# Cross-attention and routed feed-forward on one core: another order of the first transfers, all first norms on VectorE, and a query stack with its group axis first

## What is computed

```python
x = x + cross_attention(layernorm(x), ctx, ctx, mask)     # 16 heads of 8, scores clipped to +-50, no maximum taken
x = x + moe(layernorm(x))                                 # 8 experts, the best 2 of each token, 128 -> 512 -> 128, gelu

q = layernorm(x) @ W_q.T;  k = ctx @ W_k.T;  v = ctx @ W_v.T
p = exp(clip(q k / sqrt(8)));  attention = (p v / sum(p)) @ W_o.T
```

## Time and profile before

| | |
|---|---|
| median of 3 runs | 1106.81 us (1106.25 to 1107.64) |
| the profiled execution | 1106.66 us, its span 1104.9 us |
| mean granted clock of TensorE | 0.969 of full speed |
| PE busy | 1033.4 us, 94% of the span |
| ACT, DVE, POOL busy | 769.6, 761.0, 240.0 us |
| chain that ended last, PE's share | 90% |

### The profile page before, as it was taken

The page is one execution under the profiler, slowest core; times in us unless marked ns, Lnnn a source line. Parts: engine busy times, 40 slices in busy tenths (PEclk is TensorE's granted clock), DMA queues, the critical chain, the costliest instruction groups (busy, mean ns, idle before and its releaser), DMA issues.

```text
span 1104.9 us, 32396 instructions
## 1 busy us (share of the span) xinstructions
PE 1033.4 (94%) x10544; PEld 759.8 (69%) x10545; DVE 761.0 (69%) x2088; ACT 769.6 (70%) x1088; POOL 240.0 (22%) x320
## 2 busy tenths in 40 slices
PE   5789999999999999999999999999999999399990
PEld 3567677777777677777677777777767776299990
DVE  4567777777777777777777777777777777444433
ACT  2567877777777877777877777877778777144430
POOL 3331111111111111111111111111111111245554
PEclk8899999999999999999999999999999999699995
DMA  7645555455555554555455555555555544022216
GB/s 217 186 154 166 173 170 170 165 166 167 168 171 170 172 171 164 173 167 170 167 171 173 173 173 173 174 174 174 174 174 174 174 157 142 23 68 63 65 49 178
DMA packets 144319, 172.71 MB, mean 156 GB/s; under 512 B 32235, under 2 KB 88559, under 8 KB 144287
## 3 DMA queue, kind: packets, MB, share of 16 engines
q1 hardware_dynamic: 138622, 165.26, 45.4%
q0 software_dynamic: 4896, 6.63, 2.2%
q10 hardware_dynamic: 768, 0.41, 0.2%
HBM read 36.83 MB, written 22.08 MB: 53 GB/s over the span
## 4 chain that ended last, share of the span: by engine, by line
PE 90%; DMA 3%; POOL 2%; SPq 2%; DVE 1%; issue 1%; ACT 1%; ACTq 0%; POOLq 0%; DVEq 0%
PE scores L753 31%; PE o_sum L765 26%; PE scratch L687 7%; PE scratch L676 7%; PE scores L873 5%; PE scores L884 5%; PE scratch L671 4%; PE scratch L726 1%; SPq L535 1%; POOL w_sb L597 1%; PE scratch L681 1%; PE scratch L731 1%; DMA x_all<-in_x_dram 1%; DMA q_stack<-q_rep 1%; PE scratch L747 1%
## 5 line engine op out<-in xcount | busy, mean ns | idle before, releaser
L990 ACT ACTIVATE probs<-scores 128x800 f32<-128x800 f32 (+1 forms) x640 | 615.2, 975 | 160.7 <-PE scores L753 158.6
L753 PE MATMUL scores<-q_stack,k_stack 128*128 128x400 f32 x1536 | 415.2, 380 | 10.5 <-DMA q_stack<-q_rep 8.1
L1136 DVE TENSOR_SCALAR probs<-probs 128x800 f32<-128x800 f32 (+1 forms) x640 | 396.2, 654 | 25.2 <-ACT probs L990 25.0
L753 PEld LDWEIGHTS scores<-q_stack,k_stack 128*128 128x128 f32 x1536 | 249.2, 190 | 110.5 <-issue 100.9
L765 PE MATMUL o_sum<-probs,v_both 128*17 128x200 f32 x6144 | 316.3, 335 | 0.1
L765 PEld LDWEIGHTS o_sum<-probs,v_both 128*17 128x17 f32 x6144 | 151.1, 97 | 132.4 <-issue 71.9
L630 POOL DMA_INDIRECT expert_rows<-rows,row_atu x64 | 75.6, 1181 | 408.8 <-DVE row_atu L1233 361.4
L687 PE MATMUL scratch<-w_turned,ctxT 128*128 128x128 f32 x768 | 102.5, 277 | 0.0
L687 PEld LDWEIGHTS scratch<-w_turned,ctxT 128*128 128x128 f32 x768 | 101.2, 194 | 0.0
L1073 DVE COPY v_both<-scratch 128x512 f32<-128x512 f32 x93 | 64.4, 692 | 42.4 <-PE scratch L687 42.4
L1048 DVE CAST k_hi<-k_full 128x512 fp32r<-128x512 f32 (+1 forms) x93 | 38.4, 412 | 79.5 <-ACT k_full L932 79.4
(11 more groups left out here) (145 smaller groups left out, 771.1 us busy)
## 6 DMA issues: line engine op xcount, KB each, us to landing
k_stack<-k_hi SPq DMA_DIRECT2D x192, 256.0 KB, 2.5
k_stack<-k_lo SPq DMA_DIRECT2D x192, 256.0 KB, 2.6
expert_rows<-fill SPq DMA_DIRECT2D x32, 406.2 KB
xT_and_ctx<-in_ctx_dram SPq DMA_DIRECT2D x16, 704.0 KB
ctx_nat<-in_ctx_dram SPq DMA_DIRECT2D x16, 704.0 KB
q_rep<-q_parts SPq DMA_DIRECT2D x124, 50.0 KB, 1.9
q_stack<-q_rep SPq DMA_DIRECT2D x124, 50.0 KB, 1.9
v_both<-expert_rows SPq DMA_DIRECT2D x57, 65.0 KB, 1.8
```

Source lines behind the costliest of these rows:

```text
L753: last = nc.tensor.matmul(score_banks(c)[:, m, :], k_stack[p][:, g, t * P:(t + 1) * P], q_stack[p][:, :, g, :], start=True, stop=True)
L990: nc.scalar.activation(probs_of(c), score_banks(c), ACT.Exp, scale=SCALE).then_inc(exp_ready, 1)
L1136: nc.vector.tensor_scalar(chunk, chunk, LOW, HIGH, ALU.max, ALU.min).then_inc(probs_ready, 1)
```

## The change

Four things change. `x` comes in parts of 1, 3 and 4 groups in place of 2, 2 and 4. The transfers of the last third of the first keys and of the last part of `x` are issued behind the spreading of the second query, which waits for the first query's stacking. The norms of groups 4, 5 and 7 move from POOL to DVE, and the chunks in which DVE takes the late moments and norms are other ones. And `q_stack` has its axes as (group, head, query) where it had (head, group, query), so that the 400 columns of one group lie side by side for each matmul and each partition's part of a stacking transfer lies in four places.

```diff
-    DVE_NORMS = [0, 1, 2, 3, 6]
-    POOL_NORMS = [4, 5, 7]
...
-    X_PARTS = [(0, 2), (2, 4), (4, QSTEPS)]
-    LATE_MOMENTS = {3: 4, 4: 5, 5: 6, 7: 7}
-    LATE_NORMS = {10: 6}
+    X_PARTS = [(0, 1), (1, 4), (4, QSTEPS)]
+    LATE_MOMENTS = {4: 4, 6: 5, 8: 6, 11: 7}
+    LATE_NORMS = {7: 4, 9: 5, 11: 6, 14: 7}
...
-        q_stack = [sb(f"q_stack{p}", [P, HG, GROUPS, SQ], F32R) for p in range(2)]
+        q_stack = [sb(f"q_stack{p}", [P, GROUPS, HG, SQ], F32R) for p in range(2)]
...
-            def stack_keys(p, b):
+            def stack_keys(p, b, thirds=range(KSTEPS)):
 
-                for k in range(KSTEPS):
+                for k in thirds:
...
-                    sp.dma_start(q_stack[p][h * R:(h + 1) * R, h, :, :].bitcast(F32),
+                    sp.dma_start(q_stack[p][h * R:(h + 1) * R, :, h, :].bitcast(F32),
                                  q_rep[h * R:(h + 1) * R, :, :].bitcast(F32)).then_inc(q_stacked, 16)
...
             sp.wait_ge(cleared, 3)
-            stack_keys(0, 0)
+            stack_keys(0, 0, (0, 1))
+            spread_queries(1)
+            stack_keys(0, 0, (2,))
             load_x(2)
-            spread_queries(1)
...
-            for r in range(2, 4):
+            for r in range(2, QSTEPS):
                 invert_deviations(r)
-
-            def late_norm(r):
...
-                if r in DVE_NORMS:
-                    pe.wait_ge(normed_ready, QB * (DVE_NORMS.index(r) + 1))
-                else:
-                    pe.wait_ge(normed_ready_pool, QB * (POOL_NORMS.index(r) + 1))
+                pe.wait_ge(normed_ready, QB * (r + 1))
...
-                                            q_stack[p][:, :, g, :],
+                                            q_stack[p][:, g, :, :],
```

More of the change, by code:

```diff
@@ L306, in xattn_moe @@
         normed_ready = sem("normed_ready")
-        normed_ready_pool = sem("normed_ready_pool")
         w_in_psum = sem("w_in_psum")
@@ L966, in stack_first @@
                 for h in range(HG):
-                    act.dma_start(q_stack[0][h * R:(h + 1) * R, h, :, :].bitcast(F32),
+                    act.dma_start(q_stack[0][h * R:(h + 1) * R, :, h, :].bitcast(F32),
                                   q_rep[h * R:(h + 1) * R, :, :].bitcast(F32)).then_inc(q_stacked, 16)
```

## The result

The changed kernel took 1098.68 us in the median of 4 runs (1096.85 to 1099.86) against 1106.53 us of the kernel before beside it; the ratio is 0.9926 with an interval of 0.9909 to 0.9943. It is faster by 7.9 us, where 22.6 were forecast. The profiled execution took 1099.86 us, within 0.4 us of the first rival's 1100.2.

A forecast was written before the change was run, and what follows sets the result against it. PE was taken to bound the kernel, 90% of the span by the chain. From 1106.66 us, 6.5 us at the start and 16.1 us in the score matmuls came off, giving 1084.1 us; the forecast's own range was 1077 to 1095.

The forecast's parts named there:

- the first rival: Score matmuls stay at 0.185 us because the excess belongs to operand type or weights; layout idle; 1100.2 us, chance 0.36.
- the term of 16.1 us: Steady part: 1488 score matmuls each 0.012 us shorter through the new layout, 17.9 us, less a tenth.
- The query stack: Prediction's section on `q_stack`'s new axes: stacking transfers cost nothing more, score matmuls gain 16.1 us.
- the three jumps: Score matmuls read 400 columns in four pieces; without the jumps between them the distance falls 0.014 us, to 0.171 us.
- The start: Up to the second sequence: first scores at 26.9 us instead of 33.80, second sequence at 62.9 instead of 69.38.
- The term of 6.5 us: Gain at the second sequence's start from the earlier first scores; bounds 1.0 to 8.8 us.
- The first part of `x`: Halving `x` part 0 lands it sooner, so the first query follows 1.2 us earlier; bounds 0 and 2.
- Each us of landing behind 38.9 us is one us of time: First sequence: later landing of `x` part 2 costs time one for one, as DVE's 16.9 us follow whole.
- those 16.9 us: DVE's work from `x` part 2's landing at 38.9 us to the clipping of chunk 11, at 55.8 us.
- The second rival: First sequence: late `x` part 2 makes DVE wait longer than the start won; landing at 50 us gives 1111 us; chance 0.05.

The follow-up runs named there:

- the early `x` part: Changed kernel with `x` part 2 issued once the first query is stacked, ahead of second query's spreading and last third of keys: 1094.39 us.
- The bf16 kernel: Changed kernel with all score matmuls on two fixed bf16 tiles of zeros, 400 columns: 1049.33 us.
- the one with zeros in `F32R`: Changed kernel with all score matmuls on two fixed tiles of zeros of type `F32R`, 400 columns: 1098.96 us.

## Why the prediction was wrong in size

**The step that failed** is the term of 16.1 us under "The query stack", in the sentence "If the three jumps make the difference, the distance falls to 0.171 us", and the choice of 0.012 us per matmul behind it. The jumps make 0.7 ns inside a group (183.22 to 182.57), and the whole term measures about 1.4 us (0.045 us in each of 31 sequences). The excess belongs to `F32R`, as the first rival had it: 13 to 14 of its 16 ns go when the type does, and none of them with the addresses. The 0.185 us itself was read from modelled durations; the starts give 183.2 ns, an excess of 16.5 ns and not 18. The step that led there was the comparison with L687: its 0.004 us above the columns were measured on another type at two periods per column, and I took the type for equal and the layout for the difference, though they differed in both. I had written that no other line uses the type and still gave the layout 0.55.

The Trainium skill had spoken against the term, in SBUF — State Buffer, section "Specifications (TRN2)": two accesses in each 16-byte line are enough, so by it either layout reads at full speed. The trace agrees: 0.7 ns between the two layouts.

**The start was right.** First scores forecast at 26.9 us and found at 26.30 (26.09 when run again); the landing of the last `x` part at 38.9, found at 39.48; DVE's wait 3 to 5 us, found 3.82; second sequence at 62.9, found at 63.10 (62.20). The term of 6.5 us measures 6.28 us at the second sequence. The first part of `x`, taken at 1.2 us, is worth about 1 us alone.

**Inside the first sequence errors cancelled**, so the closeness of 62.9 is in part luck. I put the clipping of chunk 11 at 55.8 us, as the wait that PE ends on, and 7.5 us from PE's value matmuls to the next sequence. The clipping ended at 53.85 + 0.57 = 54.42 us, as DVE's work took 14.9 us in place of 16.9. PE did not wait for it: its value matmuls start at 54.95 us with no wait in front, 0.53 us behind, since PE was late from two earlier waits for DVE (the clipping of chunk 4 and the norm of group 4) and a clock of 0.50. From there it took 63.10 - 54.95 = 8.15 us. The kernels with the early `x` part and with the norms alone take the same 8.15 us (49.91 to 58.06, 57.29 to 65.44), so the 7.5 us of a steady sequence were too little for the first.

The claim "Each us of landing behind 38.9 us is one us of time" came close. In the kernel that lands the part early, DVE takes the first late moments 4.38 us sooner (35.10 against 39.48), PE does end on the clipping of chunk 11 (the 1.08 us at 49.91), and the second sequence comes 5.04 us sooner (63.10 to 58.06), 3.9 us in the medians.

**The norms** I costed only as work inside those 16.9 us. Alone they are the largest single part: transfers 3.4 us, norms 4.2 us, parts of `x` about 1 us, layout none that its own comparison shows. They add up to 8.6 us; the change has 7.9, with 1 to 2 us of uncertainty on each, so the times alone don't show that anything overlaps. The traces do: alone the norms shorten the first sequence by 3.94 us, beside the transfers, with `x` part 2 landing late, by 1.2.

**The second rival**, a late `x` part that costs more than the start wins, did not come true: the part was there at 39.48 us and not behind 45.4, as the forecast had it. But the place was right: with another order of the same transfers about 4 us more come back, which the forecast had booked as the price of the early start.

## What to carry to other kernels

A surplus per instruction belongs to whatever differs from the row it is compared with; when type and layout both differ, run the instruction once with the other type or the other layout before giving the surplus to either. When transfers are moved behind a critical one, order what was moved by who waits for it first: here 4 us lay in the order of transfers that were all "later". And what an edit is worth depends on what else holds the same stretch: the norms' new place gave 4.2 us alone, and about 1 beside a late `x` part.

## What the runs showed of the hardware

- A score matmul of 400 columns in `F32R` starts 182.6 ns after the one before, one in bf16 169 to 170 ns; at 300 and 512 columns `F32R` takes 139 and 231.5 ns. The bf16 kernel wins 1098.96 - 1049.33 = 49.6 us against the one with zeros in `F32R`, 32 ns for each of 1536 matmuls: more than the distance inside a group explains. The rest stands at the start of a group, where a score matmul follows another kind of matmul: its second one starts 280 ns after the first in `F32R` and 176 ns in bf16 (means, between 100 and 900 us). At 16 groups in a sequence that is 1.7 us, about as much as the whole sequence is shorter in bf16 (28.16 to 26.58 us). The `F32R` excess there is about the same at 300 columns (239 ns, 100 over the distance inside a group) and at 512 (330, 99 over), so it doesn't depend on the columns. The weight loads last 189 ns in `F32R` and 99 in bf16 on average, as the pages have it (columns as in the earlier trace rows), first with zeros in `F32R`, then in bf16:

```profile
L738 PEld LDWEIGHTS scores<-q_zero,k_zero 128*128 128x128 f32 x1536 | 247.5, 189 | 105.4 <-issue 92.2
```

```profile
L738 PEld LDWEIGHTS scores<-q_zero,k_zero 128*128 128x128 bf16 x1536 | 120.0, 99 | 147.2 <-issue 93.0
```

  That the longer load makes the longer step fits these numbers, but no run changes the weights' type alone.
- The lower clock after a wait doesn't come every time. The kernel before waited 2.82 us for POOL, was busy for 2.18 us of 55 to 60 us, and then had 0.67 from 60 to 65 us. The kernel with the new layout alone has the same wait (2.81 us) and is busy for 2.19 us of the same stretch, and keeps the full clock; its second sequence starts at 67.22 us and not 69.38. Its windows:

```profile
55.00:60.00 5.00, 2.19 (x23) 1.58 (x21) 2.87 (x5) 1.57 (x3) 4.81 (x6) 1.00 0.62 225
60.00:65.00 5.00, 4.63 (x47) 3.59 (x47) 3.32 (x5) 3.98 (x6) 4.80 (x6) 1.00 0.11 27
```

  That execution took 1102.46 us, of 1102.11 to 1108.01. The two shortest of its 11 executions have a mean granted clock of 0.974, the other nine (1105.06 us and more) one of 0.967 to 0.969. So this clock is likely what spreads the times of this kernel over 6 us; only one of the 11 was profiled, so it isn't shown.
